# Self attention by groups of 2 heads × 512 tokens, with probabilities turned in 32×32 blocks on VectorE and products with the values as four 32-row matmuls side by side

## The reference

```python
# self attention: 32 heads of 128, 8 KV heads, 576 keys: 512 from the cache, 64 new
q = rope(x @ wq.T); k = rope(x @ wk.T); v = x @ wv.T
k_full = concat([k_cache[block_idx], k]); v_full = concat([v_cache[block_idx], v])
attn = softmax(q @ k_full.T / sqrt(128)); x = ln(x + (attn @ v_full) @ wo.T)
# cross attention on ctx, with biases; then z = x W^T + b plus a scaled low rank term
x = ln(x + xattn(x, ctx)); x = ln(x + ffn(x))
```

## Time and profile before

| what | value |
|---|---|
| median of 3 runs | 3161.43 us (3159.43 to 3161.79) |
| profiled execution, its own time | 3161.03 us |
| its span | 3159.2 us (1.8 us lie around it) |
| instructions | 49966, of which 19793 matmuls |
| busy | PE 3102.2, DVE 2081.7, ACT 1490.5, POOL 776.1 us |
| DMA | 85.37 MB |

### The profile page before, as it was taken

One profiled execution on the slowest core, in us unless ns is written; L12 is line 12 of the kernel. 1 busy time (PEld: TensorE's weight loads), 2 busy tenths in 40 slices (PEclk: granted clock), 3 DMA queues, 4 the chain that ended last, 5 costly groups with the idle time before them and its releaser, 6 DMA issues.

```text
span 3159.2 us, 49966 instructions
## 1 busy us (share of the span) xinstructions
PE 3102.2 (98%) x19793; PEld 2739.0 (87%) x19793; DVE 2081.7 (66%) x4293; ACT 1490.5 (47%) x3146; POOL 776.1 (25%) x835
## 2 busy tenths in 40 slices
PE   7999999999999999999999998999999999999997
PEld 6888888888888888888888888999999999999986
DVE  5767776777776776777777676565555556555567
ACT  4455454554555555555555554443334444433344
POOL 2322322322322322322322223221212221222114
PEclk9999999999999999999999999999999999999999
DMA  2000000000000000000000002111111111111101
GB/s 92 18 15 11 18 15 11 17 15 11 18 15 14 14 15 14 14 15 14 14 18 11 11 21 61 41 37 38 45 31 44 51 47 35 41 38 38 34 18 54
DMA packets 99827, 85.37 MB, mean 27 GB/s; under 512 B 11096, under 2 KB 77192, under 8 KB 99592
## 3 DMA queue, kind: packets, MB, share of 16 engines
q1 hardware_dynamic: 97544, 77.97, 8.3%
q0 software_dynamic: 2048, 4.20, 0.4%
HBM read 77.69 MB, written 4.19 MB: 26 GB/s over the span
## 4 chain that ended last, share of the span: by engine, by line
PE 90%; DVE 3%; issue 2%; ACT 2%; POOL 2%; DMA 0%; SPq 0%; POOLq 0%; ACTq 0%; DVEq 0%
PE big L1568 55%; PE big L1658 12%; PE bank L1568 11%; PE bank L1667 9%; PE bank L1561 2%; ACT P L728 1%; DVE nmx L1158 1%; POOL P L589 1%; ACT pth L749 1%; POOL xacc L654 1%; DVE xTl L1085 0%; DVE P L1164 0%; PE big L1561 0%; DVE stat L1192 0%; DMA raw<-in_L_attn_wk 0%
## 5 line engine op out<-in xcount | busy, mean ns | idle before, releaser
L589 POOL TENSOR_SCALAR P<-P,rrec 128x640 f32<-128x640 f32 x512 | 411.6, 804 | 1367.5 <-DVE rrec L1165 1367.0
L1177 DVE TENSOR_TENSOR ptl<-bank,pth 128x512 fp32r<-128x512 f32 x640 | 439.5, 687 | 186.4 <-ACT pth L749 186.4
L728 ACT ACTIVATE P<-big,nmx 128x576 f32<-128x576 f32 x512 | 379.1, 740 | 376.9 <-DVE nmx L1158 376.9
L749 ACT ACTIVATE pth<-bank 128x512 fp32r<-128x512 f32 x512 | 304.9, 596 | 531.5 <-PE big L1568 306.4
L1568 PE MATMUL big<-xTh,wqTh 128*128 128x256 f32 (+1 forms) x1528 | 502.2, 329 | 1.7 <-DVE wqTl L1091 1.7
L1568 PE MATMUL big<-xTl,wqTh 128*128 128x256 f32 (+1 forms) x1528 | 490.2, 321 | 0.0
L1568 PE MATMUL big<-xTh,wqTl 128*128 128x256 f32 (+1 forms) x1528 | 488.9, 320 | 0.0
L1158 DVE TENSOR_REDUCE nmx<-big 128x1 f32<-128x576 f32 x512 | 385.0, 752 | 109.5 <-PE big L1658 109.3
L1667 PEld LDWEIGHTS bank<-ident,P 128*128 128x128 f32 x2560 | 320.5, 140 | 104.0 <-POOL P L589 16.4
L1667 PE MATMUL bank<-ident,P 128*128 128x128 f32 x2560 | 390.0, 273 | 9.9 <-POOL P L589 8.8
L1568 PEld LDWEIGHTS big<-xTh,wqTh 128*128 128x128 f32 x1528 | 294.0, 192 | 21.4 <-DVE wqTl L1091 2.0
(11 more groups left out here) (243 smaller groups left out, 6983.1 us busy)
## 6 DMA issues: line engine op xcount, KB each, us to landing
raw<-in_L_xattn_Wq SPq DMA_DIRECT2D x33, 256.0 KB, 2.9
raw<-in_L_attn_wq SPq DMA_DIRECT2D x32, 256.0 KB, 2.6
raw<-in_L_attn_wo SPq DMA_DIRECT2D x32, 256.0 KB, 2.8
raw<-in_L_xattn_Wo SPq DMA_DIRECT2D x32, 256.0 KB, 2.7
rawb<-in_L_xattn_Wo SPq DMA_DIRECT2D x32, 256.0 KB, 2.8
rawb<-in_L_xattn_Wq SPq DMA_DIRECT2D x31, 256.0 KB, 2.9
raw<-in_L_xattn_Wkv SPq DMA_DIRECT2D x19, 256.0 KB, 2.7
out<-xacc SPq DMA_DIRECT2D x7, 512.0 KB, 2.8
```

What stands on the lines that cost most here:

```text
L589: pool.tensor_scalar(P[:, i % 8, :], P[:, i % 8, :], rrec[:, i % 8:i % 8 + 1], 1.0, ALU.mult, ALU.mult).then_inc(p_norm(i), 1)
L728: act.activation(P[:, i % 8, 0:KEYS].rearrange("p (k n) -> p k n", k=2), ps_s[i % 2][:, :, 0:HALF], ACT.Exp, bias=nmx[:, i % 8:i % 8 + 1], ...
L749: act.activation(pth[:, k % 2], ps, ACT.Copy).then_inc(tile_hi(("p", u, j)), 1)
L1177: dve.tensor_tensor(ptl[:, k % 2], ps, f(pth[:, k % 2]), ALU.subtract).then_inc(tile_lo(("p", u, j)), 1)
```

## The change

Self attention is done in 64 groups of 2 heads × 512 tokens (`head(k, u)` = 2(k//2)+u; groups 0 to 31 take the first 1024 tokens, 32 to 63 the rest, so each head's wq and wo are loaded and split twice, 64 times each). Only `PSLOTS` = 4 tiles of P are kept.

- **Turning P.** DVE transposes each 128×576 tile in place by 32×32 blocks (`turn`, L1298). Partition 32a+j then holds key 32b+j of the tile's tokens 32a to 32a+31, for each block b of keys. PE's `turn` of P goes. ACT copies the turned tile to its high half (`turned_hi`, L905), POOL subtracts the low half (`low`, L733).
- **Values.** `values(k)` (L1766) multiplies 32 keys at a time: for each of 18 blocks and 3 terms four matmuls, one per row group a of 32 partitions, 256 columns (2 heads × 4 tiles × 32 tokens), into four PSUM banks. The 32 rows of values stand at all four row groups. There are 216 per group in place of 28; 28,800 matmuls in all in place of 19,793.
- **Normalising.** The inverses of the sums apply to the output, after `values`: DVE `invert_sums` once a group, SP writes 128×8 inverses to DRAM, waits, and reads them back to every partition (`spread_sums`), DVE multiplies (`normalise_out`, L1310, four of 128×256), ACT and POOL make the halves (L911, L738). POOL's multiplication of P and DVE's doubling copy go.
- **Layout.** The host hands over x, ctx, wq, wk, wv, wo, Wq, Wkv, W, A and the biases already transposed in blocks (`_lay_out`, `_blocks`), so PE turns none of them; x is loaded a second time in rows for the sums. Only the rotated keys, and the x of the later stages, are still turned by PE.
- **Residence.** Keys and values, split, are kept in DRAM and loaded again (`load_keys`, `early_values` and `late_values`: 4 blocks ahead, 14 after the last product with the old KV head, in 8 or 16 DMAs of 32 partitions). x of one half is swapped through DRAM at groups 30 and 31.
- **Order.** PE per k: values(k), scores 4 and 5 of group k+1, query(k+2, 0), score 6, project 0, score 7, project 1, score 0 of group k+2, query(k+2, 1), a small task, score 1, project 2, score 2, project 3, score 3.

The core of the diff:

```diff
-            def turn(u, j):
-                ps = pt_bank(("p", u, j))
-                for t in range(4):
-                    gate.wait_ge(p_norm, 4 * u + t)
-                    m = pe.transpose(ps[:, 128 * t:128 * t + 128], P[:, (4 * u + t) % 8, 128 * j:128 * j + 128],
-                                     ident[:, :])
...
-                if j < 4:
-                    terms = [(vh[:, b, j], h), (vl[:, b, j], h), (vh[:, b, j], l)]
-                else:
-                    terms = [(v4a[:, b], h), (v4b[:, b], l)]
-                products(ps_o, terms, pv_done, (u, j), first=j == 0, final=j == 4)
+                for b in range(KB):
+                    s = (KB * n + b) % VSLOTS
+                    for j, (v, p) in enumerate(((vh, pth), (vl, pth), (vh, ptl))):
+                        for a in range(4):
+                            r = slice(32 * a, 32 * a + 32)
+                            first, final = b == 0 and j == 0, b == KB - 1 and j == 2
+                            m = pe.matmul(ps_o[a][:, 0:256], v[r, s, :], p[r, lo:hi + 1:hi - lo, b, :, :], start=first,
+                                          stop=final)
...
+            def turn(i):
+
+                gate.wait_ge(exp_done, i)
+                dve.transpose(P[:, i % PSLOTS, :], P[:, i % PSLOTS, :]).then_inc(p_turned(i), 1)
...
+            def normalise_out(k, a):
+                gate.wait_ge(pv_done, k)
+                gate.wait_ge(in_r, k)
+                dve.tensor_tensor(rall_quarter(a), ps_o[a][:, 0:256].rearrange("p (u t j) -> p u t j", u=2, t=4),
+                                  rall_quarter(a), ALU.mult).then_inc(o_norm((k, a)), 1)
...
+            def turned_hi(i):
+                gate.wait_ge(p_turned, i)
+                if 2 * (i // 8) + i % 8 // 4 >= 3:
+                    gate.wait_ge(pv_done, (2 * (i // 8) + i % 8 // 4 - 3) // 2)
+                act.activation(third_columns(pth, i), blocks_of(i), ACT.Copy).then_inc(p_hi(i), 1)
...
+            def spread_sums(k):
+
+                gate.wait_ge(rec_done, k)
+                sp.dma_start(kept_r[k % 2].rearrange("t p -> p t"), normal_columns(k)[1],
+                             allow_slow_non_contiguous=True).then_inc(out_r(k), 16)
+                gate.wait_ge(out_r, k)
+                if k >= 1:
+                    gate.wait_ge(o_low, (k - 1, 3))
+                sp.dma_start(rall[:, :, :], kept_r[k % 2:k % 2 + 1].to_broadcast([128, 8, 128])).then_inc(in_r(k), 16)
```

More of the change, by code:

```diff
@@ L172, with real, sequence, part @@
[L172 to L176, removed]
-ONE_SLOT = {a: i % 3 for i, a in enumerate(ONE_LOADS)}
+def real(k):
+    return 0 <= k < GROUPS
+def sequence(k):
+    return k // 4
+def part(k):
+    return k % 2
+def slot(k, u):
+    return (2 * k + u) % 3
@@ L1704, in first_keys @@
[L1704 to L1709 removed]
+                a, b = 128 * (t % 4), 128 * (t % 4) + 128
+                terms = split3(qTh[:, u, a:b], qTl[:, u, a:b], kTh[:, n % 2], kTl[:, n % 2])
+                for j, (l, r) in enumerate(terms):
+                    for h in range(2):
+                        m = pe.matmul(ps_s[i % 2][:, h, 0:HALF], l, r[:, HALF * h:HALF * h + HALF], start=j == 0,
+                                      stop=j == 2)
+                        if j == 2 and h == 1:
+                            m.then_inc(s_done(i), 1)
@@ new lines, in project @@
+            def project(k, t):
+                a, b = 128 * t, 128 * t + 128
+                ps = out_place(out_bank(k, t), (acc_done, (k, t)))
+                gate.wait_ge(o_low, (k, 3))
+                terms = []
+                for u in range(2):
+                    n = head(k, u)
+                    wait_split(gate, "wo", n)
+                    terms += split3(oh[:, pos(k, u), a:b], ol[:, pos(k, u), a:b], woh[:, n % 3], wol[:, n % 3])
+                products(ps, terms, wo_done, (k, t))
@@ new lines, in tensor_program @@
+            for k in range(-2, GROUPS):
+                now, after, later = real(k), real(k + 1), real(k + 2)
+                if now:
+                    values(k)
+                if k == GROUPS - 1:
+                    first_keys(0)
+                    first_keys(1)
+                if after:
+                    score(8 * (k + 1) + 4)
+                    score(8 * (k + 1) + 5)
+                if later:
+                    query(k + 2, 0)
+                if k == -2:
+                    new_key(0, 1)
+                    turn_keys(0)
+                if after:
+                    score(8 * (k + 1) + 6)
+                if now:
+                    project(k, 0)
+                if after:
+                    score(8 * (k + 1) + 7)
+                if now:
+                    project(k, 1)
+                if later:
+                    score(8 * (k + 2))
+                    query(k + 2, 1)
+                for a in task(k):
+                    small_task(*a)
+                if later:
+                    score(8 * (k + 2) + 1)
+                if now:
+                    project(k, 2)
+                if later:
+                    score(8 * (k + 2) + 2)
+                if now:
+                    project(k, 3)
+                if later:
+                    score(8 * (k + 2) + 3)
@@ L2014, in tensor_program @@
                         value_rows2(g + 1, s)
-                if not early and not last:
-                    for a in work[2:]:
-                        weight2(*a)
             def low_rank(q):
@@ L2120 @@
     arrays, args = {}, []
[L2121 to L2122 removed]
+    for name, a in _lay_out(inputs):
         arrays[f"in_{name}"] = a
```

1334 lines of the change are left out of this document (621 added, 713 removed).

## The result

| | us |
|---|---|
| before, median of 4 runs | 3161.06 (3159.43 to 3161.79) |
| changed, median of 4 runs | 3083.44 (3081.69 to 3096.31) |
| ratio | 0.9761, 95% interval 0.9747 to 0.9775 |
| forecast | 2947 (2860 to 3180) |

The account below looks back on a forecast made before the run. PE, busy 98% of the span, was taken to bound the kernel, stage one being a sum of matmuls. Terms −278.4, −43.5, −4.3, +25.3, +83.2, −7 and +10 gave −214.7 from 3161.0, forecast 2947 us, range 2860 to 3180.

Parts of the forecast that it names:

- The set of four: Value products: four 32-row, 256-column matmuls side by side take 0.1175 us a set, 3456 sets, −4.3 us against before.
- Rivals 2, 3 and 4: Value sets, in order: partial overlap, 3150 us, chance 0.10; issue-bound, 3353, 0.14; one after another, 4200, 0.04.
- the 29 ns of the earlier trace: Time per instruction in cross attention's 64-row pairs, the trace's densest piece; eight at 29 ns make a set 0.235 us.
- The prices on DVE, ACT and POOL: Work per group: DVE 18.0, ACT 17.2, POOL 16.8 us, all under PE's 24.1; a turn on DVE 0.75.
- four times as full: POOL's load after the change compared with before, though it loses the 804 ns pass that scaled each tile.
- The new wait: PE idles about 1.3 us in each of 64 groups, waiting for ACT's exponential before the next group's first score: +83.2 us.
- exp6: ACT's exponential of score tile 6, forecast done 10.1 us after the last value product, with PE ready at 8.9.
- The DMAs: Inverses' trip through DRAM: at hand by 21 to 24 us, wanted at 25.4, so covered, with little left.
- The host's layout: 100 blocks of weights, x, ctx and fw no longer turned by PE, the start's apart: −43.5 us.
- Start and changes of KV head: Start, last group, KV changes and half time together: +10 us, bounds −10 and +30.
- Stages two and three: After stage one: about 10 us saved, from the turned blocks of ctx and fw that these lose.
- Rival 1: Engines behind the new wait slower (turn at 1.48 us, or inverses late): 3 us more per group, 3139 us, chance 0.12.

Follow-up runs that it names:

- e1: Changed kernel with a short write of the inverses: one more VectorE transpose, 128 pieces of 128 bytes in place of 1024 of 4; 2953.94 us.
- e2: Changed kernel with the read taken from x and issued before the unchanged write of the inverses, without normalising by the true sums; 3053.0 us, one run.
- e7: Kernel before, with only wq, wk, wv and wo handed over turned by the host, low halves made by POOL; 3169.23 us, ratio 1.0022.
- e4: Against e1: the old write of 1024 pieces of 4 bytes added to a spare place, waited for one group later; 3414.3 us, one run.
- e9: Changed kernel with the write of 1024 pieces held back until the group's last value product, in three groups of four; 3799.2 us, one run.

## Why the prediction was right and wrong

**The set of four: right.** 0.1197 us a set against 0.1175, by which 3456 sets cost 8 us more. Rivals 2, 3 and 4 fall. Eight instructions issue in 0.12 us, 15 ns each, so the 29 ns of the earlier trace rows were not a bound by issue. Of the Trainium skill's two figures in "TensorE: Matmul & The Clock Gate", neither bore on this: a set at 62 ns a MATMUL (Part 1) would be 0.248, at 3.07× (Part 3) 0.156. That the second would give 3081 us, 2 below the measured 3083, is chance: the sets cost what was forecast, and the time was lost elsewhere.

**The prices on DVE, ACT and POOL: right**, 767 ns for a turn against 750. POOL did not become "four times as full" in stage one, but 2.5 times (624 us of 960 against 250).

**The new wait: wrong, and no loss.** I had exp6 at 10.1 us and PE ready at 8.9. There is no such wait in the plain groups; the chain above has the third maximum done at 1509.54 + 0.66, 7.7 us after the scalings began, where I had 9.1. The four scalings take 1.42 us (I had 1.83); where the other 1.0 us went I did not follow up. What there is, is 0.3 to 0.4 us for the bank that add_out frees. With the short write the period is 24.71 where I said 25.4, some 45 us too much over 64 groups. By the timeline of such a period the 48 products of 512 columns take 11.03 us, the scores 6.67, the value products with the way into row groups and out 6.67, and PE is idle for 0.34: it is PE's own work, priced at 24.1 and measured at 24.37.

**The DMAs: the step that failed.** It said "the write issues in at most 2.5 and lands after another 2.5". The rows behind it were the *issue* of a 4-byte load (0.60) and the landing of a 256 KB load in large pieces (2.6); no row showed a landing of 4-byte pieces, and 2.5 was not a bound but a guess by size. Measured: 8.5 to 14.7 us, 10.2 in the median. I asked whether the trip fits into the period (21 to 24 of 25.4: "covered, with little left"; at hand at 25.8 in the chain above, though the inverses were ready at 11.0 and not 12.9) and not what follows if it does not, and not at all what 1024 pieces do to the queues beside them. e1 gives the price of this step, 129.5 us, of the 136 by which the forecast missed; e2 divides it, some 30 for the latency and 100 for the rest, with one run on the side of e2. The text also counted 7 changes of KV head; values are loaded again at 15, 8 of them from half time on. The Trainium skill, "DMA: Bandwidth & Descriptors", Specifications, has a minimum of 512 bytes for line rate, with a read-modify-write below it. Pieces of 4 and of 128 bytes both lie below it, and the write takes 10.71 us with the one and 1.53 with the other, so the limit alone does not price this trip; whether the number of pieces or their size does was not parted.

**The host's layout: not settled.** "100 turned blocks ... −43.5" counted instructions on the engine that had 98% busy. e7 shows that in the kernel before the 76 blocks of weights are worth nothing by themselves, since the wait for POOL's scaling, 14.57 us a unit, lies right beside PE's own 14.59. But the changed kernel has no such scaling, and in its plain period PE works for 24.37 of 24.71 us, so a turned block put back there should lengthen it. No run does that, so neither the 43.5 nor a nothing is shown for the change as a whole.

**Start and changes of KV head: wrong**, +10 with bounds to +30. The first value product comes at 88 us where the kernel before has its at 50, and PE idles 34.2 us ahead of it. Six changes at 36 us a group are 64 us above 25.4. Of the changes, most is the small pieces again: with the short write they fall to 28.9. The start is not: with the short write the first value product still comes at 82. Stages two and three, from the first score product of cross attention to the end, are shorter by 4.9 us, for which I had 10.

With that one step mended, the sum stands at 2953.9 against 2947. It is no proof of the sum: with the short write the start is 32 us later than before and the first 33 periods are 60 us above 24.71, for which I had 10 in all, and the waits that were too long (45 us) stand against that. The rest of the balance I did not trace.

**Rival 1** had the name of the cause in its parentheses ("or the inverses come late"), at 3139 and 0.12. The time of 3083 lies between it and the forecast, nearer to it; but lateness by itself is worth about 30 us by e2, not 192.

## What to carry to other kernels

Price a DMA by the number and size of its pieces, from a row with the same pieces, and where there is none take the range wide: here 10.2 us lay behind an issue of 0.4. Then ask two questions and not one: who waits for it, and what else uses the queues while it runs. A transpose of 0.2 us that leaves an eighth of the pieces bought 129 us here.

An engine that is 98% busy may have the next bound right beside it. Here PE's work of 14.59 us a unit hid a wait for POOL at 14.57, and 33 us of PE work could be taken away for nothing. It could be seen beforehand: the few units with less work for PE were no shorter. Look at such units before pricing a part of a change by itself, and price it again in the kernel in which it will stand, where the other chain may be gone.

## What the runs showed of the hardware that I had not expected

- Four 32-row matmuls on four row groups, 256 columns each, into four PSUM banks, go at 0.1197 us a set, as fast as one full-height product of 256 columns; eight instructions are issued in that time, for 6.4 us without a break.
- A DMA of 1024 pieces of 4 bytes from SBUF to DRAM takes 8.5 to 14.7 us, though its packets have all begun 1.7 us after the issue, in the medians. While it is under way beside dense matmuls, PE stands for up to 3.5 us at a time without any semaphore, in e4 up to 7.7. The value products of the same 48 groups take 6.47 us in e9 without it and 7.55 in the changed kernel with it.
- Beside such a write, packets of 16 KB that bring instructions last 1.96 us in the median, against 0.98 otherwise. That the stalls are these loads held up is my reading of this and of "issue"; in e4 the packets are not longer, and the stalls are. Whether the number of pieces or their size does it was not tried.
- After such stalls, and after PE's longer idle times, stretches of the value products run at the lower of the two granted clocks (1.2 GHz), with sets at 0.21 us in place of 0.12. The window from 40 to 1000 has a clock of 0.95 in the changed kernel and 0.98 with the short write; both contain the wait ahead of the first value product.
